# Two operands of VectorE's products move from SBUF to PSUM in a graph network's edge loops

## The chip, the cores and the metric

The program runs on one core of a Trainium2 chip. The metric is the device time of one execution in microseconds (us). The kernel before took 9235.6 us, the median of three executions (9228.3 to 9247.12).

The engines are named as in the profile: PE is TensorE (PEld its weight loads), DVE is VectorE, ACT is ScalarE, POOL is GpSimd and SP is SyncE.

## The reference

The input is a graph of 12,500 nodes with 256 features each, and 212,500 given edges. It runs through a graph convolution (GCN), two graph attention layers (GAT), each with a batch norm, and a mixture of eight experts. The change lies in the loops over the edges, which compute this:

```
# GCN: out[d] = sum over edges (s -> d) of h[s] * norm
# GAT, 4 heads of 64 features:
e    = alpha_s[src] + alpha_d[dst]
e    = where(e > 0, e, 0.2 * e)
w    = exp(e - emax[dst])
wsum = segment_sum(w, dst)
out  = segment_sum(w[:, :, None] / wsum[dst] * h[src], dst)
```

The kernel takes an upper bound in place of the maximum, sums the weighted rows and the weights together, and divides later. The edges are sorted by destination.

## The kernel before

The edges stand in 416 groups of 512, and a group in 4 chunks of 128, one edge per partition. Each of the three edge stages (one GCN, two GAT) runs over the 416 groups in `fast_edges`, with five engines side by side that meet at semaphores only. `any_edges` is a second way for graphs that don't fit the first, and does not run here.

What one group takes in a GAT stage:

- POOL (`gather`, L702) issues four indirect DMAs, one per chunk. Each fetches 128 rows (256 features and 4 source logits) from the table in HBM to a ring of four buffers, `rows`. Group g goes to the buffer of group g-4, so it waits until the message of group g-4 is made (`rows_used`). The indices lie in SBUF (`idx`).
- SP loads the destinations once more as a row that is spread over the partitions (`mod`).
- DVE builds two one-hot matrices in `hots`: `hot_t` from `mod` and the partition number (L795), and `hot` by comparing the counting row 0 to 127 (`count`) with the edge's destination in its window of 128 nodes (`mod_t`), for four chunks in one instruction (L796).
- PE looks up the destination's logits (`look`, L750). DVE makes the edge's logit (`logits`, L805 to L810), ACT its exponential (`weigh`, L737), and DVE multiplies the 1024 gathered features by the weights (`messages`, L818). `msg` holds the 256 products of each edge and behind them the 4 weights, which are summed like them.
- PE adds up the messages by destination with `hot` as its weights (`total`, L765), and DVE adds the sums to `feat` for two windows (`add`, L784).

A GCN stage has only the gathers, `hot` (L796), the sums and the adding.

The order on each engine is that of the code: `pace` runs each step with a lead over the turn's number and unrolls four turns into one pass of the loop. On DVE a turn t holds the message of t+1, the adding of t-1, the logits of t+2 and the one-hots of t+3. On ACT it holds the weights of t+2 and the staging of the indices of t+6. `build_edges` allocates the buffers and starts the stage. In a GAT stage DVE first multiplies every node's own row by its own weight, in a single instruction (L1002).

`general_buffers` allocates two PSUM tiles, `ps_rel` and `ps_as`, that only `any_edges` uses.

Of the kernel before, what the change touches and what calls it, by code (L numbers as in the profile page):

```python
# [22 lines left out]
P = 128  # L23
F32 = mybir.dt.float32
BF16 = mybir.dt.bfloat16
I32 = mybir.dt.int32
U32 = mybir.dt.uint32
ALU = mybir.AluOpType
ACT = mybir.ActivationFunctionType
# [3 lines left out]
HEADS, HID = 4, 64  # L33
FEAT = HEADS * HID
ROW = FEAT + HEADS
WIDE = FEAT + 2 * HEADS
CH = 4
GE = CH * P
RING = 4
# [93 lines left out]
def wait(eng, sem, count):  # L133

    if not isinstance(count, int) or count > 0:
        eng.wait_ge(sem, count)
# [532 lines left out]


def edge_buffers(T, width, gat):
    B = dict(idx=T.sb("idx", [P, RING, CH], I32), rows=T.sb("rows", [P, RING, CH, width]),
             hot=T.sb("hot", [P, RING, CH, P]), ps_sum=[T.ps(f"ps_sum{i}") for i in range(2)])
    if gat:
        B.update(mod=T.sb("mod", [P, RING, GE], BF16), hot_t=T.sb("hot_t", [P, RING, GE], BF16),
                 tab=T.sb("tab", [P, RING, 2, 24], BF16), near=T.sb("near", [P, 2, CH, 2 * HEADS]),
                 logit=T.sb("logit", [P, 2, CH, HEADS]), msg=T.sb("msg", [P, 2, CH, ROW]),
                 ps_near=[T.ps(f"ps_near{i}") for i in range(2)])
    return B


def fast_edges(L, M, K, S, B, table, mod_rows, width, gat):

    NG = S.NG
    feat = K["feat"]
    idx_staged, begun = M.sem(L + "idx_staged"), M.sem(L + "begun")
# [27 lines left out]
    def act_program(act):  # L714
        regs = [act.alloc_register(f"{L}act_w{j}") for j in range(RING)]

        def stage(i, c):

            j, g = c % RING, RING * i + c
            wait(act, rows_in[j], 64 * (i + c // RING))  # L720
            act.copy(B["idx"][:, j, :], at1(K["src_t"], g)).then_inc(idx_staged, 1)  # L721
            if not gat:
                return
            wait(act, near_made, g - 3)
            if j == 0:
                act.load(regs, K["first_w"][0:1, bass.ds(g, RING)])
            w = act.snap(regs[j], min_val=0, max_val=S.NW - 1)
            for side, mask in enumerate(("in_first", "in_next")):
                ins = act.activation(B["tab"][:, j, side, :], K["tab24"][:, bass.ds(w + side, 1), :].squeeze(1),
                                     ACT.Copy, scale=K[mask][:, one(g)])  # L730
            ins.then_inc(tab_staged, 1)

        def weigh(i, c):
            g = RING * i + c
            act.wait_ge(logit_step, 4 * g + 4)
            wait(act, summed, g - 1)
            act.activation(B["msg"][:, c % 2, :, FEAT:ROW], B["logit"][:, c % 2, :, :], ACT.Exp).then_inc(weighed, 1)  # L737

        pace(act, NG, [(weigh, 2), (stage, RING + 2)] if gat else [(stage, RING)], RING)
# [31 lines left out]
    def dve_program(dve):  # L771
        regs = [dve.alloc_register(f"{L}dve_w{j}") for j in range(RING)]

        def add(i, c):

            g, b = RING * i + c, c % 2
            if c % RING == 0:
                dve.load(regs, K["first_w"][0:1, bass.ds(g, RING)])
            w = dve.snap(regs[c % RING], min_val=0, max_val=S.NW - 1)
            dve.wait_ge(summed, g + 1)  # L780
            wait(dve, added, g)
            for side, mask in enumerate(("in_first", "in_next")):
                to = feat[:, bass.ds(w + side, 1), 0:width].squeeze(1)
                ins = dve.scalar_tensor_tensor(out=to, in0=B["ps_sum"][b][:, 0:width],  # L784
                                               scalar=K[mask][:, one(g)], in1=to, op0=ALU.mult,
                                               op1=ALU.add)
            ins.then_inc(added, 1)

        def hots(i, c):
            j, g = c % RING, RING * i + c  # L790
            wait(dve, summed, g - 3)
            if gat:
                wait(dve, near_made, g - 3)
                dve.wait_ge(mod_in[j], 16 * (i + c // RING + 1))
                dve.tensor_scalar(B["hot_t"][:, j, :], B["mod"][:, j, :], K["part"][:, 0:1], None, ALU.is_equal)  # L795
            dve.tensor_tensor(B["hot"][:, j, :, :], K["count"][:, :].unsqueeze(1).to_broadcast([P, CH, P]),  # L796
                              at1(K["mod_t"], g).unsqueeze(2).to_broadcast([P, CH, P]),
                              ALU.is_equal).then_inc(hot_built, 1)

        def logits(i, c):  # L800
            j, g, b = c % RING, RING * i + c, c % 2
            near, logit = B["near"][:, b, :, :], B["logit"][:, b, :, :]
            dve.wait_ge(near_made, g + 1)
            link = Chain(dve, logit_step, 4 * g)
            link(dve.tensor_reduce(near, B["ps_near"][b][:, 0:24 * CH].rearrange("p (c v s) -> p c v s", c=CH, s=3),  # L805
                                   AX, ALU.add))
            dve.wait_ge(rows_in[j], 64 * (i + c // RING + 1))
            link(dve.tensor_tensor(logit, B["rows"][:, j, :, FEAT:ROW], near[:, :, 0:HEADS], ALU.add))
            link(dve.scalar_tensor_tensor(out=logit, in0=logit, scalar=SLOPE, in1=logit, op0=ALU.mult, op1=ALU.max))
            dve.tensor_tensor(logit, logit, near[:, :, HEADS:2 * HEADS], ALU.subtract).then_inc(logit_step, 1)  # L810

        def messages(i, c):
            j, g, b = c % RING, RING * i + c, c % 2
            dve.wait_ge(weighed, g + 1)
            rows = B["rows"][:, j, :, 0:FEAT].rearrange("p c (h f) -> p c h f", h=HEADS)
            out = B["msg"][:, b, :, 0:FEAT].rearrange("p c (h f) -> p c h f", h=HEADS)
            w = B["msg"][:, b, :, FEAT:ROW].unsqueeze(3).to_broadcast([P, CH, HEADS, HID])
            dve.tensor_tensor(out, rows, w, ALU.mult).then_inc(msg_made, 1)  # L818

        steps = [(messages, 1), (add, -1), (logits, 2), (hots, 3)] if gat else [(add, 0), (hots, 3)]  # L820
        pace(dve, NG, steps, RING)

# [3 lines left out]
def general_buffers(T, gat):  # L826
    G = dict(rel=T.sb("rel", [P, CH]), win=T.sb("win_now", [P, 1]))
    if gat:
        G.update(relb=T.sb("relb", [P, CH, P]), hot_t=T.sb("hot_tf", [P, GE]), ps_rel=T.ps("ps_rel"),
                 ps_as=T.ps("ps_as"), asb=T.sb("asb", [P, CH, P]), top=T.sb("top", [P, 1]),  # L830
                 masked=T.sb("masked", [P, GE]))
    return G

# [132 lines left out]
def build_edges(nc, L, M, K, S, table, mod_rows, width, gat, flag):  # L966

    with ExitStack() as scope:
        T = Mem(nc, scope, L)
        B = edge_buffers(T, width, gat)  # L970
        G = general_buffers(T, gat)
        fast = fast_edges(L, M, K, S, B, table, mod_rows, width, gat)
        slow = any_edges(L, M, K, S, B, G, table, width, gat)
        begun = M.sem(L + "self_messages")

        def either(eng, one_way, other_way):
            ok = eng.value_load(flag[0:1, 0:1], min_val=0, max_val=1)
            with eng.If(ok != 0):
                one_way(eng)
            if other_way:  # L980
                with eng.Else():
                    other_way(eng)

        with nc.Block() as block:
            @block.gpsimd
            def _(pool):
                either(pool, fast["gather"], slow["gather"])

            @block.scalar
            def _(act):  # L990
                either(act, fast["act"], slow["act"] if gat else None)

            @block.tensor
            def _(pe):
                either(pe, fast["pe"], slow["pe"])

            @block.vector
            def _(dve):
                if gat:

                    body = K["feat"][:, 0:S.NW, 0:FEAT].rearrange("p w (h f) -> p w h f", h=HEADS)
                    dve.tensor_tensor(body, body, K["feat"][:, 0:S.NW, FEAT:ROW].unsqueeze(3).to_broadcast(  # L1002
                        [P, S.NW, HEADS, HID]), ALU.mult).then_inc(begun, 1)
                    dve.wait_ge(begun, 1)
                either(dve, fast["dve"], slow["dve"])

            if gat:
                @block.sync
                def _(sp):
                    either(sp, fast["send_mods"], None)  # L1010
# [1076 lines left out]
```

## Time and profile before

| | |
|---|---|
| median of three executions | 9235.6 us |
| profiled execution, its span | 10130.6 us |
| POOL busy | 6123.9 us (60%) |
| DVE busy | 5042.3 us (50%) |
| PE busy | 5027.6 us (50%) |
| ACT busy | 1644.8 us (16%) |
| all POOL gathers of the GAT stages (L702) | 3560.5 us, 3328 of them |
| all POOL gathers of the GCN stage (L702) | 1635.9 us, 1664 of them |
| mean granted clock of TensorE | 0.805 |

The profiled execution is 895 us longer than the median of those that were only timed. A row of the views gives an instruction's line, engine, operation and what it writes and reads. In the timeline a number in brackets is the time for which the engine stood idle before it, with what ended that. The three edge stages are told apart by their gathers: `gcn_rows` between 390 and 2773 us, and `gat_rows` between 2952 and 5595 us and again between 5959 and 8587 us.

### The profile page before, as it was taken

Reading aid. Unit: us, or ns where it says so; the run is one execution under the profiler, and the core shown is the slowest. Engines: PE = TensorE matmul, PEld = TensorE weight load, DVE = VectorE, ACT = ScalarE, POOL = GpSimd, SP = SyncE. Lnnn points to the kernel's source line nnn. Section 1 sums busy time; section 2 is a strip of 40 time slices with the busy share of each in tenths; the row PEclk is TensorE's granted clock in tenths of the full one; section 3 lists DMA queues with packets and bytes.
Section 4 is the critical chain, followed back from the end, with each engine's and each line's share of the span. In section 5 each row is a group of like instructions: output and inputs, shape, how many; then the busy total and the mean of one; then the engine's idle time right before and its main releaser. Section 6 shows DMA issues by size and latency. Waiting matters only on the chain. (4 is left out here: it accounts for less than half of the span.)

```text
span 10130.6 us, 119298 instructions
## 1 busy us (share of the span) xinstructions
PE 5027.6 (50%) x24975; PEld 3941.7 (39%) x24976; DVE 5042.3 (50%) x11847; ACT 1644.8 (16%) x6285; POOL 6123.9 (60%) x5675
## 2 busy tenths in 40 slices
PE   3333333333355555554555545555555555248995
PEld 3333333333323333333333333333333333246994
DVE  8511111111145555555555775555555555775335
ACT  4200000000021111111111231111111111225331
POOL 0366666666646666666666556666666666742552
PEclk9999999999977777766777777777677777657997
DMA  5311111111123443333343023333343343121225
GB/s 195 103 23 23 23 23 23 23 22 23 22 80 106 106 106 105 106 104 102 106 105 106 27 79 106 106 106 105 106 107 105 104 108 98 32 88 56 70 70 189
DMA packets 488664, 834.96 MB, mean 82 GB/s; under 512 B 119275, under 2 KB 332904, under 8 KB 481958
## 3 DMA queue, kind: packets, MB, share of 16 engines
q0 software_dynamic: 232576, 551.37, 20.8%
q1 hardware_dynamic: 242740, 270.23, 8.9%
q10 hardware_dynamic: 13298, 12.80, 0.4%
q8 instruction: 18, 0.29, 0.0%
q14 instruction: 32, 0.26, 0.0%
HBM read 751.87 MB, written 82.11 MB: 82 GB/s over the span
## 5 line engine op out<-in xcount | busy, mean ns | idle before, releaser
L702 POOL DMA_INDIRECT gat_rows<-gat_table,gat_idx x3328 | 3560.5, 1070 | 1738.8 <-issue 985.5
L765 PE MATMUL gat_ps_sum<-gat_msg,gat_hot 128*128 128x260 f32 x6656 | 2476.5, 536 | 1017.7 <-DVE feat L784 784.6
L702 POOL DMA_INDIRECT gcn_rows<-gcn_table,gcn_idx x1664 | 1635.9, 983 | 1097.9 <-issue 519.1
L765 PEld LDWEIGHTS gat_ps_sum<-gat_msg,gat_hot 128*128 128x128 f32 x6656 | 1701.2, 268 | 1401.3 <-DVE gat_msg L818 849.3
L765 PE MATMUL gcn_ps_sum<-gcn_rows,gcn_hot 128*128 128x64 f32 x3328 | 798.7, 424 | 1611.8 <-issue 702.3
L765 PEld LDWEIGHTS gcn_ps_sum<-gcn_rows,gcn_hot 128*128 128x128 f32 x3328 | 737.6, 328 | 1673.0 <-issue 1649.2
L805 DVE TENSOR_REDUCE gat_near<-gat_ps_near 128x32 f32<-128x96 f32 x832 | 212.4, 255 | 2075.1 <-remote 1930.2
L750 PE MATMUL gat_ps_near<-gat_tab,gat_hot_t 128*128 128x24 bf16 x6656 | 312.2, 179 | 1614.7 <-DVE gat_hot L796 1033.7
L784 DVE SCALAR_TENSOR_TENSOR feat<-gcn_ps_sum,in_first,feat 128x64 f32 x416 | 117.8, 283 | 1945.8 <-remote 1177.9
L750 PEld LDWEIGHTS gat_ps_near<-gat_tab,gat_hot_t 128*128 128x128 bf16 x6656 | 262.3, 102 | 1999.5 <-issue 1835.4
L818 DVE TENSOR_TENSOR gat_msg<-gat_rows,gat_msg 128x1024 f32<-128x1024 f32 x832 | 1012.8, 1217 | 0.6 <-ACT gat_msg L737 0.6
L737 ACT ACTIVATE gat_msg<-gat_logit 128x16 f32<-128x16 f32 x832 | 179.5, 216 | 4496.8 <-DVE gat_logit L810 2055.6
L796 DVE TENSOR_TENSOR gat_hot<-count,mod_t 128x512 f32<-128x512 f32 x832 | 569.7, 685 | 0.0
L721 ACT COPY gcn_idx<-src_t 128x4 int32 (+1 forms) x416 | 80.1, 193 | 2304.6 <-DMA gcn_rows<-gcn_table,gcn_idx 2271.5
L784 DVE SCALAR_TENSOR_TENSOR feat<-gat_ps_sum,in_first,feat 128x260 f32 x832 | 400.0, 481 | 2.8 <-PE gat_ps_sum L765 2.4
L1908 PE MATMUL ffn_ph<-ffn_xt,ffn_up_now 128*128 128x128 f32 x3264 | 400.0, 276 | 0.0
L784 DVE SCALAR_TENSOR_TENSOR feat<-gat_ps_sum,in_next,feat 128x260 f32 x832 | 397.4, 478 | 0.0
L1878 POOL DMA_INDIRECT y_rows<-ffn_y,ffn_row x204 | 202.6, 993 | 319.8 <-DVE ffn_y L1979 297.5
L1923 PE MATMUL ffn_py<-ffn_w,ffn_h 128*128 x1632 | 387.9, 381 | 4.7 <-DMA ffn_b2b<-in_L_ffn_b_dram 4.7
L1908 PEld LDWEIGHTS ffn_ph<-ffn_xt,ffn_up_now 128*128 128x128 f32 x3264 | 383.0, 193 | 0.1
L1869 POOL DMA_INDIRECT ffn_xg<-xn_rows,ffn_idx x204 | 198.7, 974 | 210.7 <-ACT ffn_idx L1933 145.3
L1979 DVE TENSOR_TENSOR ffn_y<-ffn_py,ffn_b2b 128x256 f32<-128x256 f32 x204 | 86.6, 425 | 475.0 <-PE ffn_py L1923 256.3
(326 smaller groups left out, 6823.8 us busy)
## 6 DMA issues: line engine op xcount, KB each, us to landing
gat_mod<-mod_rows SPq DMA_DIRECT2D x832, 128.0 KB
gi_mods<-mod_rows SPq DMA_DIRECT2D x52, 1024.0 KB, 4.7
gat_rows<-gat_table,gat_idx POOLq DMA_INDIRECT x3328
gcn_rows<-gcn_table,gcn_idx POOLq DMA_INDIRECT x1664
gat_table<-feat SPq DMA_DIRECT2D x14, 1820.0 KB, 7.3
mix_rows<-y_rows SPq DMA_DIRECT2D x98, 256.0 KB, 5.1
xn_rows<-ffi_z SPq DMA_DIRECT2D x7, 1792.0 KB, 6.7
out_dram<-feat ACTq DMA_DIRECT2D x48, 256.0 KB
```

The costliest lines, as they stand in the source:

```text
L702: pool.indirect_dma_start(B["rows"][:, c, k, :], None, table, bass.IndirectOffsetOnAxis(ap=B["idx"][:, c, k:k + 1], axis=0)).then_inc(rows ...
L737: act.activation(B["msg"][:, c % 2, :, FEAT:ROW], B["logit"][:, c % 2, :, :], ACT.Exp).then_inc(weighed, 1)
L750: mm = pe.matmul(B["ps_near"][b][:, 24 * k:24 * k + 24], B["hot_t"][:, j, k * P:(k + 1) * P], B["tab"][:, j, side, :], start=(side == 0), ...
L765: mm = pe.matmul(B["ps_sum"][b][:, 0:width], B["hot"][:, j, k, :], rhs, start=(k == 0), stop=(k == CH - 1))
L784: ins = dve.scalar_tensor_tensor(out=to, in0=B["ps_sum"][b][:, 0:width], scalar=K[mask][:, one(g)], in1=to, op0=ALU.mult, op1=ALU.add)
L796: dve.tensor_tensor(B["hot"][:, j, :, :], K["count"][:, :].unsqueeze(1).to_broadcast([P, CH, P]), at1(K["mod_t"], g).unsqueeze(2).to_broad ...
L805: link(dve.tensor_reduce(near, B["ps_near"][b][:, 0:24 * CH].rearrange("p (c v s) -> p c v s", c=CH, s=3), AX, ALU.add))
L818: dve.tensor_tensor(out, rows, w, ALU.mult).then_inc(msg_made, 1)
L1869: pool.indirect_dma_start(xg[:, j, :], None, xn_rows, bass.IndirectOffsetOnAxis(ap=idx[:, j:j + 1], axis=0)).then_inc(gathered[j], 16)
L1878: pool.indirect_dma_start(y_rows, bass.IndirectOffsetOnAxis(ap=row[:, j:j + 1], axis=0), y[:, j, :], None).then_inc(stored[j], 16)
L1908: mm = pe.matmul(ps_h[b][:, k * P:(k + 1) * P], up_now[:, b, d * HD + k * P:d * HD + (k + 1) * P], xt[:, b, d, :], start=(d == 0), stop=(d ...
L1923: mm = pe.matmul(ps_y[b][:, 0:FEAT], h[:, b, k, :], w2[:, bass.ds(e, 1), k, :].squeeze(1), start=(k == 0), stop=(k == HB - 1))
```

## The change

The counting row gets a copy in PSUM, written once at the start of each edge stage, and the comparison that builds `hot` reads that copy. In the GAT stages ACT computes the exponential twice from the same logits: first to a PSUM tile (one of the two that the other way uses, in turn), then to `msg` as before. The message multiply reads its weights from the PSUM tile. The sums still read theirs from `msg`.

```
-    B = dict(idx=T.sb("idx", [P, RING, CH], I32), rows=T.sb("rows", [P, RING, CH, width]),
+    B = dict(count=T.ps("count", (P, P)), idx=T.sb("idx", [P, RING, CH], I32), rows=T.sb("rows", [P, RING, CH, width]),
...
+def weights(B, b):
+
+    return B["weight"][b][:, 0:CH * HEADS].rearrange("p (c h) -> p c h", c=CH)
...
             wait(act, summed, g - 1)
+            act.activation(weights(B, c % 2), B["logit"][:, c % 2, :, :], ACT.Exp)
             act.activation(B["msg"][:, c % 2, :, FEAT:ROW], B["logit"][:, c % 2, :, :], ACT.Exp).then_inc(weighed, 1)
...
-            dve.tensor_tensor(B["hot"][:, j, :, :], K["count"][:, :].unsqueeze(1).to_broadcast([P, CH, P]),
+            dve.tensor_tensor(B["hot"][:, j, :, :], B["count"][:, :].unsqueeze(1).to_broadcast([P, CH, P]),
                               at1(K["mod_t"], g).unsqueeze(2).to_broadcast([P, CH, P]),
                               ALU.is_equal).then_inc(hot_built, 1)
...
-            w = B["msg"][:, b, :, FEAT:ROW].unsqueeze(3).to_broadcast([P, CH, HEADS, HID])
+            w = weights(B, b).unsqueeze(3).to_broadcast([P, CH, HEADS, HID])
             dve.tensor_tensor(out, rows, w, ALU.mult).then_inc(msg_made, 1)
...
+        if gat:
+            B["weight"] = [G["ps_rel"], G["ps_as"]]
...
             def _(dve):
+                dve.tensor_copy(B["count"][:, :], K["count"][:, :]).then_inc(begun, 1)
+                dve.wait_ge(begun, 1)
```

On ACT, in the loop of a GAT stage, one turn stood like this before (ISA rows are waits and register work):

```order
L735 ISA
L737 ACTIVATE gat_msg<-gat_logit 128x4x4
L721 ISA
L721 COPY gat_idx<-src_t 128x4
L136 REGISTER_ALU
L727 ISA
L729 ACTIVATE gat_tab<-tab,in_first 128x24
L729 ISA
L729 ACTIVATE gat_tab<-tab,in_next 128x24
```

And now, with the lines of the changed file:

```order
L740 ISA
L742 ACTIVATE gat_ps_as<-gat_logit 128x16
L743 ACTIVATE gat_msg<-gat_logit 128x4x4
L726 ISA
L726 COPY gat_idx<-src_t 128x4
L136 REGISTER_ALU
L732 ISA
L734 ACTIVATE gat_tab<-tab,in_first 128x24
L734 ISA
L734 ACTIVATE gat_tab<-tab,in_next 128x24
```

The new exponential (L742) stands ahead of the old one, whose end is what DVE's message waits for, and ahead of the copy of the indices that POOL waits for.

On DVE, in the same loop, the one-hots, the message and the adding stood like this before:

```order
L795 TENSOR_SCALAR gat_hot_t<-gat_mod,part 128x512
L796 ISA
L796 TENSOR_TENSOR gat_hot<-count,mod_t 128x512
L818 TENSOR_TENSOR gat_msg<-gat_rows,gat_msg 128x4x256
L784 ISA
L784 SCALAR_TENSOR_TENSOR feat<-gat_ps_sum,in_first,feat 128x260
```

And now:

```order
L801 TENSOR_SCALAR gat_hot_t<-gat_mod,part 128x512
L802 ISA
L802 TENSOR_TENSOR gat_hot<-gat_count,mod_t 128x512
L824 TENSOR_TENSOR gat_msg<-gat_rows,gat_ps_rel 128x4x256
L790 ISA
L790 SCALAR_TENSOR_TENSOR feat<-gat_ps_sum,in_first,feat 128x260
```

Nothing moved on DVE. Of each of the two products one source changed its place: `gat_count` and `gat_ps_rel` lie in PSUM.

## Rows read from the trace of the kernel before

**Rows 1.** Instruction groups, whole span: line, count | busy us, mean ns | idle before, by releaser.

```profile
L702 POOL DMA_INDIRECT gat_rows<-gat_table,gat_idx x3328 | 3560.5, 1070 | 1738.8 <-issue 985.5 <-DVE gat_msg L818 703.5 <-ACT gat_idx L721 49.8
L702 POOL DMA_INDIRECT gcn_rows<-gcn_table,gcn_idx x1664 | 1635.9, 983 | 1097.9 <-issue 519.1 <-ACT gcn_idx L721 351.2 <-remote 227.6
L818 DVE TENSOR_TENSOR gat_msg<-gat_rows,gat_msg 128x1024 f32<-128x1024 f32 x832 | 1012.8, 1217 | 0.6 <-ACT gat_msg L737 0.6
L796 DVE TENSOR_TENSOR gat_hot<-count,mod_t 128x512 f32<-128x512 f32 x832 | 569.7, 685 | 0.0
L737 ACT ACTIVATE gat_msg<-gat_logit 128x16 f32<-128x16 f32 x832 | 179.5, 216 | 4496.8 <-DVE gat_logit L810 2055.6 <-DVE gat_logit L808 804.1 <-DVE gat_near L805 735.8
L1979 DVE TENSOR_TENSOR ffn_y<-ffn_py,ffn_b2b 128x256 f32<-128x256 f32 x204 | 86.6, 425 | 475.0 <-PE ffn_py L1923 256.3 <-issue 218.7
```

**Rows 2.** Line 702 by edge stage: duration in ns, min/median/max, first and last start.

```profile
L702 POOL DMA_INDIRECT gcn_rows<-gcn_table,gcn_idx x1664: 940/944/1815, 390.5 to 2772.5; - x185
L702 POOL DMA_INDIRECT gat_rows<-gat_table,gat_idx x1664: 940/946/25591, 2952.5 to 5595.0; - x185
L702 POOL DMA_INDIRECT gat_rows<-gat_table,gat_idx x1664: 940/946/25356, 5959.3 to 8586.6; - x185
```

**Rows 3.** Timeline, opening of the first GAT stage: start, length in us.

```profile
2950.75 26.29 DVE L1002 TENSOR_TENSOR feat<-feat 128x25088 f32<-128x25088 f32 x1 [0.30 <-PEq L1086]
2952.51 25.59 POOL L702 DMA_INDIRECT gat_rows<-gat_table,gat_idx  x1 [13.66 <-ACT gat_idx L721]
...
2981.17 0.95 POOL L702 DMA_INDIRECT gat_rows<-gat_table,gat_idx  x1 [0.30 <-issue]
...
2984.67 0.22 ACT L737 ACTIVATE gat_msg<-gat_logit 128x16 f32<-128x16 f32 x1 [30.81 <-DVE gat_logit L810]
...
2984.82 0.69 DVE L796 TENSOR_TENSOR gat_hot<-count,mod_t 128x512 f32<-128x512 f32 x1
2984.92 1.40 POOL L702 DMA_INDIRECT gat_rows<-gat_table,gat_idx  x1 [0.30 <-issue]
...
2985.42 1.22 DVE L818 TENSOR_TENSOR gat_msg<-gat_rows,gat_msg 128x1024 f32<-128x1024 f32 x1
...
2986.63 0.95 POOL L702 DMA_INDIRECT gat_rows<-gat_table,gat_idx  x1 [0.30 <-issue]
...
2990.37 1.43 POOL L702 DMA_INDIRECT gat_rows<-gat_table,gat_idx  x1 [0.30 <-issue]
```

**Rows 4.** Timeline, second GAT stage: three gathers and the DVE instruction each starts in.

```profile
6076.59 0.48 DVE L784 SCALAR_TENSOR_TENSOR feat<-gat_ps_sum,in_first,feat 128x260 f32 x1
6076.66 0.95 POOL L702 DMA_INDIRECT gat_rows<-gat_table,gat_idx  x1 [0.30 <-issue]
...
6153.76 1.22 DVE L818 TENSOR_TENSOR gat_msg<-gat_rows,gat_msg 128x1024 f32<-128x1024 f32 x1
6153.96 1.84 POOL L702 DMA_INDIRECT gat_rows<-gat_table,gat_idx  x1 [0.30 <-issue]
...
6234.04 0.42 DVE L795 TENSOR_SCALAR gat_hot_t<-gat_mod,part 128x512 bf16<-128x512 bf16 x1
6234.14 0.95 POOL L702 DMA_INDIRECT gat_rows<-gat_table,gat_idx  x1 [0.30 <-issue]
```

**Rows 5.** Timeline, early GCN stage.

```profile
400.14 0.94 POOL L702 DMA_INDIRECT gcn_rows<-gcn_table,gcn_idx  x1 [0.30 <-issue]
400.21 0.68 DVE L796 TENSOR_TENSOR gcn_hot<-count,mod_t 128x512 f32<-128x512 f32 x1
...
422.69 0.19 ACT L721 COPY gcn_idx<-src_t 128x4 int32 x1 [4.80 <-DMA gcn_rows<-gcn_table,gcn_idx]
...
427.57 0.28 DVE L784 SCALAR_TENSOR_TENSOR feat<-gcn_ps_sum,in_first,feat 128x64 f32 x1 [16.71 <-remote]
...
428.19 1.27 POOL L702 DMA_INDIRECT gcn_rows<-gcn_table,gcn_idx  x1 [2.15 <-issue]
```

**Rows 6.** Windows: PE, PEld, DVE, ACT and POOL busy us (x count), clock, DMA share, GB/s.

```profile
4000.00:4500.00 500.00, 251.39 (x1255) 180.50 (x1256) 283.71 (x702) 66.19 (x312) 331.51 (x317) 0.71 0.39 105
```

More of the change, by code:

```diff
@@ L1003, in _ @@
                         [P, S.NW, HEADS, HID]), ALU.mult).then_inc(begun, 1)
-                    dve.wait_ge(begun, 1)
+                    dve.wait_ge(begun, 2)
                 either(dve, fast["dve"], slow["dve"])
```

## The prediction

> **What bounds the kernel now.** I read the instruction groups first. The three edge stages, from 390 to 8587 us of the span, hold 4992 gathers on POOL [rows 1, 2]. In 500 us of a GAT stage POOL is busy for 331.5 us and DVE for 283.7, PE for 251.4, ACT for 66.2 [rows 6]. POOL's busy time leaves out a gap of 0.30 us before each gather (issue, which comes with every one), so the gathers start 0.94 + 0.30 = 1.25 us apart when nothing holds them. The 317 gathers of that window then take 317 x 1.35 = 429 us of its 500. POOL is the engine that sets the pace: four gathers are a group, 5.0 us at the least.
>
> The rest of the 500 us are waits of POOL for the message that frees a buffer, 703.5 us in both GAT stages, and 227.6 us of the like in the GCN stage (remote), 931.1 us in all [rows 1]. I do not take these for the kernel's own. In the GCN rows DVE stands still for 16.71 us and is let go at 427.57 us, while ACT has the rows of a group at 422.69 us as regularly as before: the rows had landed, DVE was late with something that no row names, and POOL paid 2.15 us for it [rows 5]. The profiled execution is 10130.6 - 9235.6 = 895.0 us longer than the timed median, nearly what these waits add up to. So I read the timed execution as the profiled one without them, 10130.6 - 931.1 = 9199.5 us, which the median misses by 36. There POOL is never short of a buffer and its gathers follow each other through all three stages.
>
> **What holds a gather.** Half of the gathers take 946 ns or less, but the mean in the GAT stages is 1070 ns [rows 1, 2]. The timeline shows which are long. A gather that starts at 2984.92 us, 0.10 us into the one-hot product (L796), takes 1.40 us and ends 0.81 us after that product. One that starts at 6153.96 us, inside the message product (L818), takes 1.84 us and ends 0.82 us after it [rows 3, 4]. The first gather of the stage starts inside L1002, the 26.29 us product of two SBUF operands, and takes 25.59 us [rows 3]. A gather that starts inside L784, which reads PSUM and SBUF, takes its ordinary 0.95 us, and so does one that starts inside L795, with one tensor from SBUF [rows 4]. So a gather is held to the end of a DVE instruction that reads two tensors from SBUF, and by no other. After the change neither L796 nor L818 is one.
>
> The Trainium skill says the same in "SBUF — State Buffer", section "SBUF: two separate sides": DVE and GpSimd share one pair of ports as an exclusive lock, which a DVE operation takes in a 2-port perf mode or with two SBUF inputs. The trace agrees on the two inputs. On the perf mode it does not: L795, one 16-bit source in SBUF, is what "VectorE: DVE Perf Modes" (section "What auto-detection actually checks") puts in a 2-port mode, and it held no gather here; it took 0.42 us itself. The rival on it is below.
>
> **The change part by part.**
>
> 1. *The holds in the GAT stages go.* They are 3560.5 - 3328 x 0.946 = 412.2 us. The first gathers of both stages have 25.59 + 25.36 - 2 x 0.95 = 49.1 us of it [rows 2, 3]; L1002 stays, and the DVE work of the stage waits for it anyway, so nothing comes of these. 363.1 us are left, 0.44 us per group. The undisturbed opening of the stage gives a second reading: one gather in each group is held, for 1.40 - 0.95 = 0.45 us and 1.43 - 0.95 = 0.48 us, and the next one starts just as the message ends, unharmed (2986.63 us against 2985.42 + 1.22) [rows 3]. At 0.47 us, 832 groups make 391 us. I take the middle, 377 us.
> 2. *The holds in the GCN stage go.* They are 1635.9 - 1664 x 0.944 = 65.1 us [rows 1, 2]. In the undisturbed opening the one-hot starts just behind a gather's start and holds nothing (400.21 after 400.14, that gather takes 0.94 us) [rows 5]. The held ones come where DVE catches up, which I expect little of in a timed execution. I take 0, and keep 65 us as the bound.
> 3. *The product's own length.* No row has DVE multiply with a broadcast PSUM operand. The nearest is L1979, PSUM and SBUF: 425 ns for 256 elements. The two SBUF products give (1217 - 685) / 512 = 1.04 ns per element, so 419 ns for 256 [rows 1]. PSUM costs 6 ns. At the other end stands twice the length, 685 + 1217 ns more per group; a gain is bounded at nothing, since the rate per element is the same in all three rows. I take 6 ns, that of the same operation. It lies beside POOL: DVE has 283.7 us in 79 groups, 3.6 us of a group that takes 5.
> 4. *The second exponential.* 832 x 0.22 = 180 us on ACT [rows 1]. In the opening the exponential starts at 2984.67 and the message at 2985.42 us, behind the one-hot [rows 3]. Two of them end at 2985.11, 0.3 us before that. It costs nothing; without that cover it would be 0.22 us on DVE's chain, which isn't the bound. The copy of the indices comes 0.22 us later as well. POOL needs them for the group whose buffer the message frees, and the message ends 1.5 us later still.
> 5. *The copy of the counting row* is three DVE copies of 128 elements and a wait, under 1 us each.
>
> **What is late next.** With 4.99 us per group POOL remains the bound if the buffers come back in time. The last gather of the first group starts at 2981.17 us and its message ends at 2986.64 [rows 3], 5.5 us later. POOL comes back to that buffer after 1.25 + 3 x 5.0 = 16.2 us. 10.8 us are to spare. DVE with 3.6 us and PE with 251.4 / 79 = 3.2 us per group are below 5.0 as well [rows 6].
>
> **The sum.** 9235.6 - 377 = 8858.6, and with half of the few us that the GCN stage may give I forecast 8855 us. Against the profiled execution the same holds are worth 363 + 65 = 428 us, but there I expect less: DVE's standstills remain, and a POOL that runs faster between them waits longer at each. I expect its span to fall to 9750 to 10000 us.
>
> **The rivals.**
>
> - *POOL's waits belong to the timed execution too.* For it: no row names the cause of DVE's standstills, and 895 against 931 may be chance. Then what a gather saves is partly waited off at the next standstill. With half of it lost the time is 9235.6 - 377 / 2 = 9047 us.
> - *The change does not do what it says.* The hold may hang on the operation and not on where its operands lie (L784 is another operation), or on the first operand only. If both hold as before, the time stays at 9236 us. If only the one-hot is free, the fourth gather of a group, 5.0 us after the last of the group before, falls into the message, which ends at 5.47; it then takes 5.47 + 0.82 - 5.0 = 1.29 us, 0.34 too many, and 0.12 us per group or 100 us remain as gain: 9136 us.
> - *L795 takes over as the one that holds.* It starts 0.26 us before the one-hot; with the gathers on another phase one may start in it each time. It could be held for 0.35 - 0.12 = 0.23 us, 191 us in all: 9046 us. That is the half of the page's rule on perf modes. The row against it is the gather at 6234.14 us [rows 4].
> - *DVE becomes the bound, and the kernel slower.* If a broadcast operand from PSUM comes at half the rate, DVE's group is 3.6 + 0.69 + 1.22 = 5.5 us, and the second exponential is then no longer covered: 5.7 us. It decides from 5.44 us on, what a group takes now. (5.7 - 5.44) x 832 = 216, so 9452 us. Against it stands L1979 at full rate.
>
> **How the numbers follow.** The forecast has 73%, the waits 11%, no effect 6%, the one-hot alone 3%, L795 2%, DVE as the bound 5%. The lowest time is with 391 + 65 us gone, 8780, and I set 8770. Upward the range reaches past the two cases at 9046, to 9100. What is left out is about 16%, and a little at the lower end. A measurement of this kernel tells 0.2% (18 us) from no change. Faster by more than that: 0.73 + 0.11 + 0.03 + 0.02 less a little for waits that take back everything, 0.87. Same: 0.07. Slower: 0.06.
>
> **What would show it.** In the profile after, the gathers of the GAT stages must have a mean of 0.95 to 0.98 us with the two of 25 us still there, and no gather that starts inside L802 or L824 may be long. L802 and L824 must last 0.69 and 1.22 us. ACT has 832 instructions of 0.2 us more, and no message waits for ACT. POOL waits longer in total for the messages than 703.5 us. The prediction is wrong if gathers still end 0.8 us after a product, if the products grow, or if the time gained in timed executions is well under what the gathers lost in length.

## The result, and the profile after

| | before | after |
|---|---|---|
| timed, median | 9237.1 us (9228.3 to 9247.1, 4 runs) | 8765.2 us (8763.6 to 8765.8, 4 runs) |
| ratio | 1 | 0.9481, 95% interval 0.947 to 0.9493 |
| span of the profiled execution | 9227.5 us (a second one, below) | 8763.9 us |
| span of the profiled execution shown first | 10130.6 us | |

The kernel is 471.9 us faster, 5.2%. The forecast was 8855 us with a range from 8770 to 9100: the direction and the main mechanism came out, but the time lies 5 us below the whole range.

The profiled execution now lasts as long as the timed ones. The one of before that the prediction was made from did not, so I had the unchanged kernel profiled once more (E0 below). Rows of before are read from there where a difference of some us matters.

The instruction groups of the whole span after the change (count | busy us, mean ns | idle before), answering to [rows 1]:

```profile
L707 POOL DMA_INDIRECT gat_rows<-gat_table,gat_idx x3328 | 3202.9, 962 | 1040.1 <-issue 902.4 <-ACT gat_idx L726 91.8 <-DVE gat_msg L824 46.0
L707 POOL DMA_INDIRECT gcn_rows<-gcn_table,gcn_idx x1664 | 1570.3, 944 | 857.8 <-issue 506.2 <-ACT gcn_idx L726 350.9 <-PE gcn_ps_sum L771 0.6
L802 DVE TENSOR_TENSOR gat_hot<-gat_count,mod_t 128x512 f32<-128x512 f32 x832 | 566.5, 681 | 0.1
L824 DVE TENSOR_TENSOR gat_msg<-gat_rows,gat_ps_as 128x1024 f32<-128x1024 f32 x416 | 503.0, 1209 | 0.8 <-ACT gat_msg L743 0.8
L742 ACT ACTIVATE gat_ps_rel<-gat_logit 128x16 f32<-128x16 f32 x416 | 77.9, 187 | 1805.4 <-DVE gat_logit L816 1788.3 <-PE gat_ps_sum L771 17.2
L743 ACT ACTIVATE gat_msg<-gat_logit 128x16 f32<-128x16 f32 x832 | 165.6, 199 | 0.0
```

L707 is the gather that was L702. Its mean in the GAT stages is 962 ns where [rows 1] have 1070. Over 946 ns each, 54.6 us are left: 50.0 in the first gathers of the two stages (25.93 and 26.00 us long), and some 5 us in gathers held by L801, which are below. The two products (L802, L824) last 681 and 1209 ns, no longer than before. ACT has one exponential more, and the message product waits for ACT 0.8 us in all. POOL's idle time has not grown: 1040.1 us, 0.31 per gather, where the first profile had 1738.8 and the second of before 1040.6.

A GAT group in the middle of the stage (start, length in us), answering to [rows 3, 4]:

```profile
4002.88 0.35 DVE L801 TENSOR_SCALAR gat_hot_t<-gat_mod,part 128x512 bf16<-128x512 bf16 x1
4003.14 0.68 DVE L802 TENSOR_TENSOR gat_hot<-gat_count,mod_t 128x512 f32<-128x512 f32 x1
4003.74 1.21 DVE L824 TENSOR_TENSOR gat_msg<-gat_rows,gat_ps_rel 128x1024 f32<-128x1024 f32 x1
4003.75 0.94 POOL L707 DMA_INDIRECT gat_rows<-gat_table,gat_idx  x1 [0.30 <-issue]
...
4005.00 0.94 POOL L707 DMA_INDIRECT gat_rows<-gat_table,gat_idx  x1 [0.30 <-DVE gat_msg L824]
```

The gather at 4003.75 starts 0.01 us into the message product and takes 0.94 us. It has ended 0.26 us before the product ends. Before, such a gather ended 0.82 us after it [rows 4]. It is so for all: 426 gathers of the GAT stages start while an L802 runs and 806 while an L824 runs, and the longest of them takes 0.96 us.

The same 500 us as in [rows 6], after the change and then in the second profile of before (PE, PEld, DVE, ACT, POOL busy us with counts, clock, DMA share, GB/s):

```profile
4000.00:4500.00 500.00, 311.26 (x1600) 224.68 (x1600) 357.36 (x900) 88.17 (x500) 378.47 (x400) 0.79 0.52 133
```

```profile
4000.00:4500.00 500.00, 309.93 (x1442) 218.03 (x1441) 319.07 (x810) 76.34 (x360) 390.21 (x361) 0.72 0.46 120
```

400 gathers in 500 us are 1.25 us each: 100 groups at exactly 5.0 us, the floor that the prediction gave. Before there were 361, a group in 5.54 us. POOL's busy time fell although it did more gathers.

### The profile page after: what moved, and what is told of

It reads as the page before. It is cut to its first block and busy times, and to the rows that moved or that the text cites. A ratio compares the mean times of both kernels' runs of the same rounds, so it can differ in the third digit from the quotient of the medians.

```text
span 8763.9 us, 120133 instructions
## 1 busy us (share of the span) xinstructions
PE 4960.7 (57%) x24975; PEld 3898.8 (44%) x24976; DVE 4991.6 (57%) x11850; ACT 1673.4 (19%) x7117; POOL 5700.4 (65%) x5675
## 3 DMA queue, kind: packets, MB, share of 16 engines
q0 software_dynamic: 232576, 551.37, 24.7%
## 5 line engine op out<-in xcount | busy, mean ns | idle before, releaser
L707 POOL DMA_INDIRECT gat_rows<-gat_table,gat_idx x3328 | 3202.9, 962 | 1040.1 <-issue 902.4
L771 PE MATMUL gat_ps_sum<-gat_msg,gat_hot 128*128 128x260 f32 x6656 | 2395.4, 522 | 1113.4 <-DVE feat L790 1109.1
L771 PEld LDWEIGHTS gat_ps_sum<-gat_msg,gat_hot 128*128 128x128 f32 x6656 | 1641.9, 259 | 1487.5 <-DVE gat_msg L824 1132.6
L707 POOL DMA_INDIRECT gcn_rows<-gcn_table,gcn_idx x1664 | 1570.3, 944 | 857.8 <-issue 506.2
L814 DVE TENSOR_TENSOR gat_logit<-gat_rows,gat_near 128x16 f32<-128x16 f32 x832 | 148.8, 179 | 1134.9 <-DMA gat_rows<-gat_table,gat_idx 1129.7
L802 DVE TENSOR_TENSOR gat_hot<-gat_count,mod_t 128x512 f32<-128x512 f32 x832 | 566.5, 681 | 0.1
L824 DVE TENSOR_TENSOR gat_msg<-gat_rows,gat_ps_as 128x1024 f32<-128x1024 f32 x416 | 503.0, 1209 | 0.8 <-ACT gat_msg L743 0.8
L824 DVE TENSOR_TENSOR gat_msg<-gat_rows,gat_ps_rel 128x1024 f32<-128x1024 f32 x416 | 503.1, 1209 | 0.0
L742 ACT ACTIVATE gat_ps_rel<-gat_logit 128x16 f32<-128x16 f32 x416 | 77.9, 187 | 1805.4 <-DVE gat_logit L816 1788.3
L742 ACT ACTIVATE gat_ps_as<-gat_logit 128x16 f32<-128x16 f32 x416 | 77.9, 187 | 1603.1 <-DVE gat_logit L816 1595.4
```

Of the source, the lines that this page charges most:

```text
L707: pool.indirect_dma_start(B["rows"][:, c, k, :], None, table, bass.IndirectOffsetOnAxis(ap=B["idx"][:, c, k:k + 1], axis=0)).then_inc(rows ...
L742: act.activation(weights(B, c % 2), B["logit"][:, c % 2, :, :], ACT.Exp)
L771: mm = pe.matmul(B["ps_sum"][b][:, 0:width], B["hot"][:, j, k, :], rhs, start=(k == 0), stop=(k == CH - 1))
L802: dve.tensor_tensor(B["hot"][:, j, :, :], B["count"][:, :].unsqueeze(1).to_broadcast([P, CH, P]), at1(K["mod_t"], g).unsqueeze(2).to_broad ...
```

## The experiments

### E0: the unchanged kernel, profiled again

No edit. It settles whether the 895 us between the profiled and the timed execution belong to the kernel.

> The kernel before once more, with a new profile. It asks where DVE's standstills come from. Theory A (they come from this kernel's work, and POOL waits for them in a timed execution as well): the new profile shows them again, POOL waits some 900 us in total for messages and sums, and the span is about 10,130 us, while timed executions stay at 9,237. Theory B (they were of that one profiled execution only): the span of the new profile is within 20 us of the timed time, 9,237 us, POOL's waits for messages are under 100 us, and the gathers' held time is larger than the 363 + 65 us that the first profile shows, near the 472 us that the change saved.

Measured: 9229.4 us timed, span 9227.5 us. Cores, instruction groups, and a GAT stretch of this execution:

```profile
core 0: 9227.5 us, clock 0.806
```

```profile
L702 POOL DMA_INDIRECT gat_rows<-gat_table,gat_idx x3328 | 3637.2, 1093 | 1040.6 <-issue 1011.3 <-ACT gat_idx L721 28.2 <-DVE gat_msg L818 1.2
L702 POOL DMA_INDIRECT gcn_rows<-gcn_table,gcn_idx x1664 | 1604.7, 964 | 857.8 <-issue 506.5 <-ACT gcn_idx L721 351.0 <-PE gcn_ps_sum L765 0.3
L795 DVE TENSOR_SCALAR gat_hot_t<-gat_mod,part 128x512 bf16<-128x512 bf16 x832 | 294.9, 354 | 4.0 <-DVE feat L1002 1.5
```

```profile
4001.72 0.68 DVE L796 TENSOR_TENSOR gat_hot<-count,mod_t 128x512 f32<-128x512 f32 x1
4002.32 1.22 DVE L818 TENSOR_TENSOR gat_msg<-gat_rows,gat_msg 128x1024 f32<-128x1024 f32 x1
...
4002.64 1.71 POOL L702 DMA_INDIRECT gat_rows<-gat_table,gat_idx  x1 [0.30 <-issue]
...
4007.80 1.21 DVE L818 TENSOR_TENSOR gat_msg<-gat_rows,gat_msg 128x1024 f32<-128x1024 f32 x1
4008.41 1.43 POOL L702 DMA_INDIRECT gat_rows<-gat_table,gat_idx  x1 [0.30 <-issue]
```

POOL's waits for the message are 1.2 us in all, not 703.5, and the 227.6 us in the GCN stage are gone. So they were that one execution's. The gathers, on the other hand, are held for longer than in [rows 1]. Over 946 ns each they have 3637.2 - 3148.3 = 489 us in the GAT stages, 440 of it without the two first gathers, and over 944 ns each 34 us in the GCN stage. Together that is 474 us. The change gained 472, with some 5 us of holds left.

Counting, over both GAT stages, which instruction each long gather ended 0.82 us behind gives 344 held by the one-hot (157 us), 488 by the message (274 us) and some 10 us by L795. The products hold exactly one gather in each of the 832 groups, 0.52 us per group. In the first profile the same count gives one in 638 of the 832 groups, 362 by the one-hot (140 us) and 280 by the message (224 us; a few groups have two). The gather at 4002.64 us is the kind that the opening of the stage does not show: it starts inside the message product and ends 0.81 us behind it.

### E1: only the counting row in PSUM

```diff
-            act.activation(weights(B, c % 2), B["logit"][:, c % 2, :, :], ACT.Exp)
...
-            w = weights(B, b).unsqueeze(3).to_broadcast([P, CH, HEADS, HID])
+            w = B["msg"][:, b, :, FEAT:ROW].unsqueeze(3).to_broadcast([P, CH, HEADS, HID])
```

(against the changed kernel)

> Of the change only the counting row in PSUM (all three stages); no second exponential, and the message multiply reads its weights from msg in SBUF. Theory 'held by position in time': with the one-hot free, the gather that it held goes on and the fourth one of a group falls into the message multiply, which still has two SBUF operands and ends 5.47 us after the last gather of the group before; it is held for 0.34 us, so a group falls from 5.56 to about 5.34 us: 9,237 - 180 = 9,060 us, plus up to 65 us from the GCN stage (9,000). Theory 'each product holds its own share' (holds are independent of each other, in proportion to length x length / 2): the one-hot has 0.69 squared of 0.69 squared + 1.22 squared, a quarter of the GAT gain of some 410, plus the GCN's 65: 9,070. Theory 'the operand's place does not matter': 9,237.

Measured: 9176.6 us (9176.4 to 9177.3), ratio 0.9933 (0.9914 to 0.9951). The gathers, by stage, and one of them:

```profile
L707 POOL DMA_INDIRECT gat_rows<-gat_table,gat_idx x3328 | 3618.3, 1087 | 1040.8 <-issue 1013.0 <-ACT gat_idx L726 27.9
L707 POOL DMA_INDIRECT gcn_rows<-gcn_table,gcn_idx x1664 | 1570.4, 944 | 857.6 <-issue 506.5 <-ACT gcn_idx L726 350.8 <-PE gcn_ps_sum L770 0.3
```

```profile
4006.76 1.22 DVE L823 TENSOR_TENSOR gat_msg<-gat_rows,gat_msg 128x1024 f32<-128x1024 f32 x1
4007.37 1.43 POOL L707 DMA_INDIRECT gat_rows<-gat_table,gat_idx  x1 [0.30 <-issue]
```

The gain is 57 us against before's 9233.3: 34 us are the GCN stage, whose gathers are all ordinary now (944 ns), and 19 us the GAT stages. The one-hot holds no gather there any more, but the message takes over nearly all of them: it holds 829 gathers in the 832 groups, for 0.50 us each. Both expectations of a gain were too good: 9060 (9000 with the GCN stage) and 9070 us.

### E2: only the weights in PSUM

```diff
-                dve.tensor_copy(B["count"][:, :], K["count"][:, :]).then_inc(begun, 1)
-                dve.wait_ge(begun, 1)
...
-            dve.tensor_tensor(B["hot"][:, j, :, :], B["count"][:, :].unsqueeze(1).to_broadcast([P, CH, P]),
+            dve.tensor_tensor(B["hot"][:, j, :, :], K["count"][:, :].unsqueeze(1).to_broadcast([P, CH, P]),
```

(against the changed kernel)

> Of the change only the second exponential to PSUM and the message multiply that reads it; the one-hot still compares two SBUF operands. Theory 'held by position in time': the one-hot held the gather in each group before, and still does, 0.46 us per group: no gain, 9,237 us (9,180 at the least). Theory 'each product holds its own share': three quarters of the GAT gain, 9,237 - 310 = 8,930 us. The GCN stage gains nothing in either.

Measured: 8960.7 us (8957.1 to 8971.1), ratio 0.9697 (0.9679 to 0.9715).

```profile
L707 POOL DMA_INDIRECT gat_rows<-gat_table,gat_idx x3328 | 3368.4, 1012 | 1040.5 <-issue 864.9 <-ACT gat_idx L726 145.4 <-DVE gat_msg L824 30.2
L707 POOL DMA_INDIRECT gcn_rows<-gcn_table,gcn_idx x1664 | 1615.3, 971 | 857.5 <-issue 506.2 <-ACT gcn_idx L726 350.7 <-PE gcn_ps_sum L771 0.6
L801 DVE TENSOR_SCALAR gat_hot_t<-gat_mod,part 128x512 bf16<-128x512 bf16 x832 | 331.3, 398 | 3.9 <-DVE feat L1010 1.5
```

A gain of 273 us. The expectation that the one-hot goes on holding a gather in each group (9237) fell; the other, that each product holds its own share (8930), missed by 31 us, but the same theory missed E1 by 107. The one-hot is half as long as the message product and catches fewer: 543 gathers in 832 groups, 0.31 us each, 0.20 us per group on average. One part alone gives 57 us, the other alone 273, and both together 472, more than the sum of 330. A gather that one product lets go reaches the next, so each part is worth more as the second one than alone: the one-hot 57 us alone and 195 behind the weights, the weights 273 alone and 411 behind the one-hot.

### E3: the changed kernel with both copies in SBUF

```diff
-    B = dict(count=T.ps("count", (P, P)), idx=...
+    B = dict(count=T.sb("count", [P, P]), idx=...
...
-            B["weight"] = [G["ps_rel"], G["ps_as"]]
+            B["weight"] = [T.sb(f"weight{i}", [P, CH * HEADS]) for i in range(2)]
```

It keeps the copy, the second exponential and the separate tiles, and changes only where they lie.

> The changed kernel's instructions one for one, the second exponential and the copied counting row too, but both copies lie in SBUF instead of PSUM. If the place of the operand is the cause: all of the gain is gone, 9,237 us, gathers held as before with a mean of 1.05 to 1.10 us, and the second exponential costs nothing. If the separate weights tile or the second exponential were the cause (the multiply no longer reads the tile it writes): it is as fast as the changed kernel, 8,765 us. If the second exponential costs something on the path: above 9,250 us.

Measured: 9233.6 us (median of 10), ratio to before 0.9997 (0.9987 to 1.0007).

```profile
L707 POOL DMA_INDIRECT gat_rows<-gat_table,gat_idx x3328 | 3635.6, 1092 | 1040.2 <-issue 1012.1 <-ACT gat_idx L726 27.2 <-DVE gat_msg L824 0.9
L824 DVE TENSOR_TENSOR gat_msg<-gat_rows,gat_weight 128x1024 f32<-128x1024 f32 x832 | 1011.7, 1216 | 0.8 <-ACT gat_msg L743 0.8
L742 ACT ACTIVATE gat_weight<-gat_logit 128x16 f32<-128x16 f32 x832 | 179.5, 216 | 3840.4 <-DVE gat_logit L816 3831.0 <-PE gat_ps_sum L771 9.4
```

The gathers are back at 3635.6 us, E0's figure within 2 us, and so is the time. The whole gain hangs on the memory in which one operand of each product lies, the first of the one-hot and the second of the message; the second exponential, 179.5 us of ACT, costs nothing.

### E4: the self product reads PSUM too

```diff
+                    own = G["ps_rel"][:, 0:S.NW * HEADS].rearrange("p (w h) -> p w h", h=HEADS)
+                    dve.tensor_copy(own, K["feat"][:, 0:S.NW, FEAT:ROW]).then_inc(begun, 1)
+                    dve.wait_ge(begun, 2)
-                    dve.tensor_tensor(body, body, K["feat"][:, 0:S.NW, FEAT:ROW].unsqueeze(3).to_broadcast(
-                        [P, S.NW, HEADS, HID]), ALU.mult).then_inc(begun, 1)
-                    dve.wait_ge(begun, 2)
+                    dve.tensor_tensor(body, body, own.unsqueeze(3).to_broadcast(
+                        [P, S.NW, HEADS, HID]), ALU.mult).then_inc(begun, 1)
+                    dve.wait_ge(begun, 3)
```

(against the changed kernel)

> The changed kernel, and in it also the product at the start of each GAT stage (every node's row by its own weight, 26.3 us) reads its weights from a PSUM copy. The prediction put its hold of the first gather, 25 us per stage, at nothing, since DVE's work waits for that product anyway. Theory 'POOL sets the end of the stage': the gathers of the first four groups go out during the product; POOL then waits for the first message, some 4 us after the product, and issues the fifth group there, while now it has four groups of 5.0 us to issue first, less the one gather that was held: about 15 us per stage are gained, 8,765 - 30 = 8,735 us. Theory of the prediction (DVE's work waits anyway): 8,765 us.

Measured: 8742.4 us (8740.0 to 8748.3, 5 runs), ratio to before 0.9461 (0.9448 to 0.9473). Opening of the first GAT stage:

```profile
2649.43 26.29 DVE L1015 TENSOR_TENSOR feat<-feat,gat_ps_rel 128x25088 f32<-128x25088 f32 x1
2650.26 1.19 POOL L707 DMA_INDIRECT gat_rows<-gat_table,gat_idx  x1 [13.66 <-ACT gat_idx L726]
2651.75 0.95 POOL L707 DMA_INDIRECT gat_rows<-gat_table,gat_idx  x1 [0.30 <-issue]
...
2669.26 0.94 POOL L707 DMA_INDIRECT gat_rows<-gat_table,gat_idx  x1 [0.30 <-issue]
2681.58 0.94 POOL L707 DMA_INDIRECT gat_rows<-gat_table,gat_idx  x1 [11.38 <-DVE gat_msg L824]
```

The product of 26.29 us no longer holds the first gather. POOL meanwhile issues 16 gathers, which fill the ring of four groups, stops, and waits 11.38 us for DVE. So 24.7 us of hold (25.93 - 1.19) become 11.1 us of wait beyond the usual gap: the 17th gather of a stage starts 31.3 us after the first, where it was 45.0 us after the change, 13.7 us per stage and 27 in both. The product itself is no shorter. The profiled spans differ by 18.5 us: the rest of the two GAT stages is 5.8 us longer than after, the GCN stage 1.9 us, and why is open. This is the fastest version: its median is 22.8 us under the one of after, and no run of either reaches into the other's. The two were timed beside different runs of before; by the ratios the difference is 0.9481 - 0.9461, 18 us, and their intervals overlap by 0.0003.

### E5 and E6: the message product in pieces, all in SBUF

```diff
-            rows = B["rows"][:, j, :, 0:FEAT].rearrange("p c (h f) -> p c h f", h=HEADS)
-            out = B["msg"][:, b, :, 0:FEAT].rearrange("p c (h f) -> p c h f", h=HEADS)
-            w = B["msg"][:, b, :, FEAT:ROW].unsqueeze(3).to_broadcast([P, CH, HEADS, HID])
-            dve.tensor_tensor(out, rows, w, ALU.mult).then_inc(msg_made, 1)
+            for k in range(0, CH, CH // n):          # n = 2 (E5) or 4 (E6)
+                v = slice(k, k + CH // n)
+                rows = B["rows"][:, j, v, 0:FEAT].rearrange("p c (h f) -> p c h f", h=HEADS)
+                out = B["msg"][:, b, v, 0:FEAT].rearrange("p c (h f) -> p c h f", h=HEADS)
+                w = B["msg"][:, b, v, FEAT:ROW].unsqueeze(3).to_broadcast([P, CH // n, HEADS, HID])
+                ins = dve.tensor_tensor(out, rows, w, ALU.mult)
+            ins.then_inc(msg_made, 1)
```

(against before)

> The kernel before with the message multiply cut in two instructions of 512 elements, everything in SBUF. Theory 'a gather is held to the end of the instruction in which it starts': the longest hold of a gather falls from 1.1 to 0.5 us, the mean hold per group from 0.51 to about 0.30 us, 9,233 - 175 = 9,060 us. Theory 'a start in a two-operand product costs what it costs, whatever the length' (arbitration, not a lock for the instruction): 9,233 us, or some us more for the longer DVE chain.

> The same with four instructions of 256 elements. Held to the end of the instruction: the hold in a message piece is 0.2 us at the most, that of the one-hot stays; 0.20 us per group, 9,233 - 260 = 8,970 us; near the kernel with the weights alone in PSUM (8,960). Cost independent of the length: 9,233 us or more, and if several pieces in a row keep POOL out (no turn for it between them) the hold is as long as before as well, 9,233 us.

Measured: two pieces 8991.6 us (8986.9 to 9000.0), ratio 0.9728 (0.9713 to 0.9743); four pieces 9025.1 us (9021.0 to 9027.3), ratio 0.9764 (0.9749 to 0.9779). Two pieces, then four:

```profile
L702 POOL DMA_INDIRECT gat_rows<-gat_table,gat_idx x3328 | 3397.7, 1021 | 1041.2 <-issue 1001.1 <-ACT gat_idx L721 40.0
L820 DVE TENSOR_TENSOR gat_msg<-gat_rows,gat_msg 128x512 f32<-128x512 f32 x1664 | 1070.8, 683 | 0.6 <-ACT gat_msg L737 0.6
```

```profile
L702 POOL DMA_INDIRECT gat_rows<-gat_table,gat_idx x3328 | 3423.1, 1029 | 1041.1 <-issue 865.8 <-ACT gat_idx L721 135.7 <-DVE gat_msg L820 39.6
L820 DVE TENSOR_TENSOR gat_msg<-gat_rows,gat_msg 128x256 f32<-128x256 f32 x3328 | 1184.0, 415 | 0.6 <-ACT gat_msg L737 0.6
```

```profile
3999.38 0.69 DVE L796 TENSOR_TENSOR gat_hot<-count,mod_t 128x512 f32<-128x512 f32 x1
3999.58 1.31 POOL L702 DMA_INDIRECT gat_rows<-gat_table,gat_idx  x1 [0.31 <-issue]
3999.98 1.42 DVE L820 TENSOR_TENSOR gat_msg<-gat_rows,gat_msg 128x256 f32<-128x256 f32 x4
4001.19 1.03 POOL L702 DMA_INDIRECT gat_rows<-gat_table,gat_idx  x1 [0.30 <-issue]
```

A hold lasts until 0.82 us behind the end of one instruction, so shorter instructions hold for less. The order of the steps stays as it was; the message's busy time grows from 1012 to 1071 and 1184 us. Two pieces gained 250 us, more than the 175 expected. Four were expected to gain 260 and gained 216. The last rows, of four pieces, show how they lose: the gather at 3999.58 us is held by the one-hot, and the next, at 4001.19 us, still meets a last quarter. Counted over both GAT stages, the two pieces hold 691 gathers (170 us) and the one-hot 70 (23 us); the four pieces hold 794 (85 us), but the one-hot 450 (138 us). The gathers' time differs by 3423.1 - 3397.7 = 25 us, nearly all of the 27 us between the two profiled spans (8998.2 and 9025.5); the medians differ by 34. So shorter pieces halve their own holds and leave the gathers to the one-hot.

## Why the prediction was right, and where it was off

**What failed** is the size of a term: the holds in the GAT stages, taken as 377 us, measured 440, and those in the GCN stage, taken as about 4, measured 34. The mechanism of the main terms held. One reading of it was wrong, that no other instruction than the two-operand products holds a gather (L795, below), and that was worth some 5 us.

**The bound** was right. POOL's gathers set the pace through all three stages, and the floor of 5.0 us per group was reached.

**The waits of POOL** were read rightly as not the kernel's own, and E0 shows it. The rival at 9047 us is refuted. The step after that was wrong: the forecast took out the waits, but sized the holds from the same disturbed execution, as if the standstills left them alone. A DVE that stands still is out of step with POOL afterwards, and meets fewer gathers: its products held one in 638 of 832 groups there, and in all 832 in E0.

**Part 1, the holds in the GAT stages,** was the term mis-sized: 363 us from the profile, 391 from the opening, 377 taken, and 440 in E0. After the change some 5 us of them are left (3202.9 - 3148.3 - 50.0). The second reading should have given the alarm, since it lay above the first. It fell short itself because two opening groups show only gathers held by the one-hot (0.45 and 0.48 us), and later more than half of the held gathers are the message's (488 of 832), at a mean of 0.56 us. The low end of the range came from the same readings, so it lay too high as well. With E0's holds the sum is 9235.6 - 440 - 34 + 5 = 8767 us, 2 us from the measured time.

**Part 2, the holds in the GCN stage,** was taken as 0 with 65 us as its bound. It was 34: 1604.7 - 1570.3. Of the 92 us by which the gain was underestimated (472 against 380), 63 belong to part 1 (440 - 377) and 30 to part 2 (34 less the 4 forecast); the 5 us still held go the other way.

**Parts 3 to 5** were right. The products with a PSUM operand take 681 and 1209 ns against 689 and 1216 in E0, so the 6 ns of cost did not come. Of the one-hot's 8 ns, though, the operand's place gives nothing: with both operands in SBUF it takes 681 ns in E2 as well, and E0's mean is higher because 114 of its 832 last 0.70 to 0.75 us, those in whose start a gather starts. DVE could not become the bound: that rival is refuted. The second exponential was covered (E3).

**The self product (L1002),** of whose holds "nothing comes", was worth 18 to 23 us when E4 freed it. The step overlooked that POOL can work ahead of DVE by 16 gathers, so that a gather held at the start delays all that follow.

**The rival that the hold hangs on the operation or on the first operand** is refuted by E3 against the changed kernel: the first operand moved in one product and the second in the other, and both holds went. Its milder form, only the one-hot free, was priced at a gain of 100 us in the GAT stages, and E1 measured 19 there (57 with the GCN stage). There the prediction let a gather of each group drift into the message for 0.34 us; in fact nearly each group had a gather in it, and 0.50 us of hold.

**L795** did not take over, but the prediction read wrongly that it holds no gather. Two places of the profile after the change, where it is L801:

```profile
3211.98 0.35 DVE L801 TENSOR_SCALAR gat_hot_t<-gat_mod,part 128x512 bf16<-128x512 bf16 x1
3212.08 1.07 POOL L707 DMA_INDIRECT gat_rows<-gat_table,gat_idx  x1 [0.30 <-issue]
...
3807.06 0.94 POOL L707 DMA_INDIRECT gat_rows<-gat_table,gat_idx  x1 [0.30 <-issue]
...
3807.53 0.60 DVE L801 TENSOR_SCALAR gat_hot_t<-gat_mod,part 128x512 bf16<-128x512 bf16 x1
```

The gather at 3212.08 us takes 1.07 us and ends 0.82 us behind L801, as with the products. In the profiles of before, E0 and after, every gather that starts 0.10 to 0.20 us into this instruction is held like this (19, 146 and 83 of them, at least 0.967 us long). One that starts up to 0.096 us into it takes its ordinary 0.95 us, and the instruction is longer instead, up to 0.42 us. The gather at 6234.14 us in [rows 4] is of this kind, at the very edge: the 0.42 us of its L795 were the sign. The hold is small because the instruction is short: in both GAT stages 5 to 7 us after the change, by how it is counted, and some 10 in E0, where the rival priced 191. So both halves of the rule that the prediction takes from "SBUF — State Buffer" of the Trainium skill ("SBUF: two separate sides") are borne out here, that on two SBUF inputs and that on the perf mode.

**The profiled execution** was expected at 9750 to 10000 us with POOL's waits above 703.5 us. It was 8763.9 us with 46.0, in 151 waits of no more than the usual 0.3 us: the disturbance did not come again in any profile.

## What to carry to other kernels

Where indirect DMAs on GpSimd set the pace, look for long DVE instructions that read two tensors from SBUF, and put the small or broadcast operand in PSUM; if there is no room, cut the longest such instruction in two. One that reads a single 16-bit tensor from SBUF holds them as well (L795), but here it was too short to matter. Free all of them, since what one lets go the next one catches: judged alone, the first part done here seemed worth 57 us and was part of 472. And if a profiled execution is some per cent longer than the timed ones, take a second before any term is sized from it: its odd waits can be subtracted, but what they did to the phase of the engines cannot.

## What the runs showed of the hardware that was not expected

- One gather per group was held by a product, in 832 of 832 groups in E0 and in E3, and in E1, with the one-hot free, 829 gathers: in E1 it simply came to the other product.
- A gather is made longer only by an instruction that ends more than 0.13 us after the gather's start (0.946 - 0.82). The products of the logits read two tensors from SBUF too, but last 0.17 to 0.18 us, and none of the 249 gathers that start while one runs after the change (L814, L816) is longer than 0.96 us.
- The hold goes the other way as well. An L801 that starts 0.46 to 0.70 us into a gather lasts 0.37 to 0.60 us instead of 0.35 and ends 1.06 to 1.07 us after the gather's start, as at 3807.53 us (158 of 832 after the change). One that starts in the first 0.46 us of a gather lasts its ordinary 0.35 us, so a gather keeps it out only late in its own time. With 65 more that a gather meets in their first 0.1 us, this makes L801's mean of 380 ns, against 354 in E0, where the gathers fall elsewhere, and 398 in E2.
- ACT writes its exponential of 16 elements to PSUM in 187 ns and to SBUF in 216 ns (E3), and the second one right behind it takes 199 ns, after the change and in E3. The Trainium skill says that ScalarE is closer to PSUM ("Advanced Engine Details and Errata", section "The Read-Write Bubble"). It says there too that VectorE is closer to SBUF; the two products that read one operand from PSUM were no longer for it (681 and 1209 ns).
- DVE's standstills and the 895 us of the first profiled execution were in none of the eight profiles taken later. Their cause is open.
